# Token tiles in lots of two behind 32 turns of the identity, the slot table moved, and four combine masks stored elsewhere

## What is computed

```
xn = layernorm(x)
q  = (xn @ Wq + bq).reshape(b, h, t, dh)      # layer 0: 16 heads of 128, causal
x  = x + attn(q, k, v) @ Wo + bo + (xn @ W.T + bias + lora experts chosen by a router)
xn = layernorm(x)
# layer 1: small attention over the batch axis, and 32 experts, 4 a token, 32 slots each
shared = silu(xn @ Wsg) * (xn @ Wsu) @ Wsd * sigmoid(xn @ Wse)
xe     = tokens gathered into the slots;  ye = (silu(xe @ Wg) * (xe @ Wu)) @ Wd
out    = x + attention + shared + sum over a token's slots of weight * ye
```

## Time and profile before

| | us |
|---|---|
| median of three runs (442.76 to 443.11) | 442.82 |
| the profiled execution's own time | 443.39 |
| its span | 441.4 |
| PE busy in the span | 422.6 |
| DVE busy | 308.0 |
| ACT busy | 245.7 |
| POOL busy | 165.4 |

### The profile page before, as it was taken

The page is one execution under the profiler, slowest core; times in us unless marked ns, Lnnn a source line. Parts: engine busy times, 40 slices in busy tenths (PEclk is TensorE's granted clock), DMA queues, the critical chain, the costliest instruction groups (busy, mean ns, idle before and its releaser), DMA issues.

```text
span 441.4 us, 8830 instructions
## 1 busy us (share of the span) xinstructions
PE 422.6 (96%) x3054; PEld 377.6 (86%) x3054; DVE 308.0 (70%) x906; ACT 245.7 (56%) x670; POOL 165.4 (37%) x293
## 2 busy tenths in 40 slices
PE   2999999899999999999999999999999989999897
PEld 1788889799999999999999999899998766577797
DVE  4645675678787888887877776657688985387442
ACT  3464563577777878786967686333314613553130
POOL 3050001455555555545555530101166005999000
PEclk9999999999999999999999999999999999999999
DMA  6920011141010100101000000000099932999002
GB/s 188 225 87 1 2 48 50 51 142 50 0 50 2 35 15 12 38 1 51 1 0 3 1 1 0 26 13 12 25 313 298 310 87 67 284 299 235 1 13 83
DMA packets 41979, 34.45 MB, mean 78 GB/s; under 512 B 6689, under 2 KB 40145, under 8 KB 41937
## 3 DMA queue, kind: packets, MB, share of 16 engines
q1 hardware_dynamic: 41552, 32.85, 26.5%
q0 software_dynamic: 384, 1.05, 0.8%
HBM read 31.80 MB, written 2.10 MB: 77 GB/s over the span
## 4 chain that ended last, share of the span: by engine, by line
PE 93%; DVE 3%; ACT 2%; issue 1%; DMA 1%; POOL 0%; DVEq 0%
PE bank L921 22%; PE bank L923 22%; PE bank L922 22%; PE bank L1079 5%; PE bank L1091 3%; PE bank L1070 3%; PE bank L1312 2%; PE bank L1279 2%; PE bank L1323 2%; PE bank L1324 2%; PE bank L1121 2%; PE bank L1299 2%; DVE GT L1787 1%; PE bank L1228 1%; DMA X<-in_L_attn_x 1%
## 5 line engine op out<-in xcount | busy, mean ns | idle before, releaser
L581 POOL TENSOR_TENSOR arena<-arena,rinv 128x384 f32<-128x384 f32 x64 | 53.0, 828 | 82.0 <-DVE rinv L1565 82.0
L921 PE MATMUL bank<-XTl,WA 128*128 128x512 f32 x128 | 54.3, 424 | 2.6 <-POOL WA L548 1.7
L923 PE MATMUL bank<-XTh,WA 128*128 128x512 f32 x128 | 51.3, 401 | 0.0
L922 PE MATMUL bank<-XTh,WA 128*128 128x512 f32 x128 | 51.3, 401 | 0.0
L746 ACT ACTIVATE PT<-bank 128x256 fp32r<-128x256 f32 x64 | 24.5, 382 | 34.1 <-PE bank L1079 34.1
L1569 DVE TENSOR_TENSOR PT<-bank,PT 128x256 fp32r<-128x256 f32 x64 | 27.2, 425 | 19.7 <-ACT arena L747 19.7
L921 PE MATMUL bank<-WA,XTh 128*128 128x256 f32 x128 | 38.4, 300 | 0.6 <-DVE K L1540 0.6
L572 POOL CAST Q<-arena 128x128 fp32r<-128x128 f32 x64 | 18.7, 292 | 48.4 <-PE bank L923 48.4
L922 PE MATMUL bank<-WA,XTl 128*128 128x256 f32 x128 | 35.7, 279 | 0.0
L923 PE MATMUL bank<-WA,XTh 128*128 128x256 f32 x128 | 35.7, 279 | 0.0
L1557 DVE CUSTOM_DVE_ANT_0 arena<-bank,posm 128x128 f32<-128x128 f32 x64 | 18.1, 282 | 20.9 <-PE bank L923 20.9
(11 more groups left out here) (327 smaller groups left out, 1449.8 us busy)
## 6 DMA issues: line engine op xcount, KB each, us to landing
arena<-in_L_ffn_Wg SPq DMA_DIRECT2D x6, 704.0 KB, 8.4
arena<-in_L_ffn_Wu SPq DMA_DIRECT2D x6, 704.0 KB, 10.5
arena<-in_L_ffn_Wd SPq DMA_DIRECT2D x6, 512.0 KB, 7.8
arena<-in_L_attn_Wq SPq DMA_DIRECT2D x4, 512.0 KB, 6.5
arena<-in_L_attn_Wk SPq DMA_DIRECT2D x8, 256.0 KB, 2.7
arena<-in_L_attn_Wv SPq DMA_DIRECT2D x8, 256.0 KB, 3.2
arena<-in_L_attn_Wo SPq DMA_DIRECT2D x1, 2048.0 KB, 8.6
arena<-in_L_ffn_Wd SPq DMA_DIRECT2D x6, 192.0 KB, 7.6
```

Of the source, the lines that this page charges most:

```text
L581: pool.tensor_tensor(pr, pr, r[:, :, None].to_broadcast([P, 3, P]), ALU.mult).then_inc(s_p, 1)
L921: pe.matmul(dst, wh, xl, start=start, stop=False)
L922: pe.matmul(dst, wl, xh, start=False, stop=False)
L923: return pe.matmul(dst, wh, xh, start=False, stop=stop)
```

## The change

Seven edits, in the order of the code. (1) SP loads Wq's first two quarters in two halves each, and pieces 2 and 3 of x behind the first quarter and the bias vectors. (2) Layer norm, token turns and the splits XTh and XTl go by lots of two tiles, both feature chunks together; `stats_of` is cut into `stats_of` and `variances`. (3) PE turns the identity 32 times into bank 7 before anything else. (4) The first four query blocks are made for tokens 0 to 255 in three parts as the operands come (`first_queries`), then for tokens 256 to 511 (`queries(0)` to `queries(3)`, matmuls of 256 columns); Q_AT puts group 1's first half ahead of group 0's second. POOL takes both low halves of the first weights. (5) The router's hidden layer comes after block 11 (before: 7); ACT's R1Th follows `q_copy(10)`, DVE's R1Tl follows `q_copy(11)`. (6) `slots_of(7)` stands ahead of `shared_product(7)`, the table's copies and turn ahead of the last shared blocks, `g_low(5)` and the two last `sum_products` behind it; block 11 comes between slots 0 and 1. (7) GT's eight masks get homes of their own (two in the products' old place, one in the place of XTl's end, one over the token numbers IT), so that masks 4, 5, 6 and 7 are made earlier; shared_down(0) stands between turn(2) and down(2). Left out below: semaphores, the functions' new bodies that only rename half to lot.

```diff
+Q_AT = [(g, half, blk) for g, half in ((0, 0), (1, 0), (0, 1), (1, 1), (2, 0), (2, 1), (3, 0), (3, 1)) for blk in range(4)]
+Q_FREE = {2: 12, 3: 16, 4: 24, 5: 32}
+CHUNKS = 4
+WARM = 32
...
-EXPERT_STEPS = [("shared", (8, 1)), ("table", 0)]
-EXPERT_STEPS += [("shared", (q, k)) for q in (9, 10, 11) for k in range(2)]
-EXPERT_STEPS += [("slots", 0), ("slots", 1), ("up", 0), ("slots", 2), ("up", 1), ("turn", 0), ("slots", 3), ("up", 2),
-                 ("down", 0), ("turn", 1), ("slots", 4), ("up", 3), ("down", 1), ("turn", 2), ("down", 2), ("turn", 3), ("sd", 0),
-                 ("weigh", 0), ("split", 0), ("down", 3), ("split", 1), ("sd", 1), ("split", 2), ("split", 3),
+EXPERT_STEPS = [("table", 0), ("shared", (8, 1))] + [("shared", (q, k)) for q in (9, 10) for k in range(2)]
+EXPERT_STEPS += [("slots", 0), ("shared", (11, 0)), ("shared", (11, 1)), ("slots", 1), ("up", 0), ("slots", 2), ("up", 1), ("turn", 0),
+                 ("slots", 3), ("up", 2), ("down", 0), ("turn", 1), ("slots", 4), ("up", 3), ("down", 1), ("turn", 2), ("sd", 0),
+                 ("down", 2), ("turn", 3), ("mask", (4, 5)), ("weigh", 0), ("split", 0), ("sd", 1), ("down", 3), ("split", 1),
+                 ("split", 2), ("split", 3),
                  ("up", 4), ("slots", 5), ("split", 4), ("sd", 2), ("split", 5), ("turn", 4), ("split", 6), ("sd", 3),
-                 ("down", 4), ("mask", 0), ("up", 5), ("slots", 6), ("mask", 2), ("sd", 4), ("turn", 5), ("sd", 5), ("down", 5),
-                 ("mask", 4), ("high", 0), ("up", 6), ("slots", 7), ("high", 3), ("low", 0), ("sd", 6), ("turn", 6), ("mask", 6),
-                 ("sd", 7), ("low", 3), ("add", 7), ("down", 6), ("mix", 0), ("mix", 1), ("up", 7), ("mix", 2), ("turn", 7),
+                 ("mask", (6,)), ("down", 4), ("mask", (0,)), ("up", 5), ("slots", 6), ("mask", (1, 2)), ("sd", 4), ("turn", 5),
+                 ("mask", (3,)), ("sd", 5), ("mask", (7,)), ("down", 5),
+                 ("high", 0), ("up", 6), ("slots", 7), ("high", 3), ("low", 0), ("sd", 6), ("turn", 6), ("low", 3),
+                 ("sd", 7), ("add", 7), ("down", 6), ("mix", 0), ("mix", 1), ("up", 7), ("mix", 2), ("turn", 7),
...
-        GT = nc.alloc_sbuf_tensor_at("GT", [P, GR, N], FR, offset=at0)
+        GT = [nc.alloc_sbuf_tensor_at(f"GT{g}", [P, N], FR, offset=at)
+              for g, at in enumerate([at0 + 4 * N * k for k in range(4)] + [at0 + 4 * (28672 + N * k) for k in range(2)]
+                                     + [at_xt + 4 * (5 * C * N // 2), at1 + 4 * 2944])]
...
+            def load_x(b):
                 sp.dma_start(X[:, 2 * b:2 * b + 2, :], x_t[:, b]).then_inc(s_x[b], 16)
-                if b == 1:
-                    sp.dma_start(WQv[:, 0], wq_t[:, :, 0:512]).then_inc(s_wq[0], 16)
+
+            def load_wq_halves(g):
+                for c in range(C):
+                    sp.dma_start(WQv[:, g, c], wq_t[:, c, 512 * g:512 * g + 512]).then_inc(s_wq[g] if c else s_wqa[g], 16)
+
+            load_x(0)
+            load_x(1)
+            load_wq_halves(0)
             for i, n in enumerate(("bq", "bk", "bv")):
                 sp.dma_start(VB[16 * i:16 * i + 16, :], row(a["L0_attn_" + n], H)).then_inc(s_vb, 16)
+            load_x(2)
+            load_x(3)
+            load_wq_halves(1)
...
+            pool.wait_ge(s_wh, 1)
+            pool.tensor_tensor(WA[:, 0, 1, 512:1024], WQ[:, 512:1024], WA[:, 0, 0, 512:1024].bitcast(F32), ALU.subtract).then_inc(s_wl, 1)
...
+            deviations(0)
+            first_high(0, 0)
+            tokens_high(0)
+            deviations(1)
+            first_high(0, 1)
+            tokens_high(1)
+            first_high(1, 0)
+            deviations(2)
+            first_high(1, 1)
+            act.wait_ge(s_vc, 2)
+            q_copy(0)
+            deviations(3)
+            q_copy(2)
+            tokens_high(2)
+            q_copy(4)
+            tokens_high(3)
+            q_copy(6)
+            q_copy(8)
+            q_copy(10)
...
+            act.wait_ge(s_t, 2)
+            act.wait_ge(s_pad, 3)
+            nc.scalar.activation(R1Th[:, :, 0:HID], pb[5][:, 0:2 * HID].rearrange("p (c n) -> p c n", c=C), ACT.Copy).then_inc(s_tc, 1)
+            nc.scalar.activation(R2T[0:HID, :], pb[5][0:HID, 256:256 + E0], ACT.Copy).then_inc(s_tc, 1)
+            for g in range(1, 4):
...
-            silu(8)
...
-                if what == "shared" and n[1] == 0:
+                if what == "shared" and (n[1] == 0 or n[0] == 8):
...
+            def first_queries(i, c, part):
+                xs = slice(T * i, T * i + T)
+                for blk in range(4):
+                    wh, wl = (WA[:, 0, k].rearrange("p (c n) -> p c n", c=C)[:, c, P * blk:P * blk + P] for k in range(2))
+                    w, x = ((wh, XTh), (wh, XTl), (wl, XTh))[part]
+                    pe.matmul(pb[blk][:, xs], w, x[:, c, xs], start=(c == 0 and part == 0), stop=(c == C - 1 and part == 2))
...
+            for _ in range(WARM):
+                pe.transpose(pb[7][:, 0:P], ident[:], ident[:])
             tokens_turn(0)
+            pe.wait_ge(s_w0, 1)
+            pe.wait_ge(s_xth, 1)
+            first_queries(0, 0, 0)
+            pe.wait_ge(s_xtl, 1)
+            first_queries(0, 0, 1)
+            pe.wait_ge(s_w0, 2)
+            first_queries(0, 0, 2)
             tokens_turn(1)
-            queries(0)
-            queries(1)
-            queries(2)
+            pe.wait_ge(s_wh, 1)
+            first_queries(0, 1, 0)
+            first_queries(0, 1, 1)
+            pe.wait_ge(s_wl, 1)
+            first_queries(0, 1, 2)
+            pe.wait_ge(s_vb, 48)
+            pe.transpose(pb[6][:, 0:48], VB, ident[0:48, 0:48]).then_inc(s_t, 1)
+            for n in range(5):
+                queries(n)
             tokens_turn(2)
+            queries(5)
             tokens_turn(3)
-            pe.wait_ge(s_vb, 48)
-            pe.wait_ge(s_xtl, 1)
-            pe.transpose(pb[4][:, 0:48], VB, ident[0:48, 0:48]).then_inc(s_t, 1)
-            queries(3)
+            queries(6)
+            queries(7)
             router_turn()
-            for n in range(4, 8):
+            for n in range(8, 12):
                 queries(n)
             router_hidden()
-            for n in range(8, 16):
+            for n in range(12, 16):
                 queries(n)
...
             stats_of(0)
+            variances(0)
+            stats_of(1)
             norm(0)
+            variances(1)
             tokens_low(0)
+            norm(1)
+            stats_of(2)
             tokens_low(1)
-            dve.wait_ge(s_wh, 1)
-            nc.vector.tensor_tensor(WA[:, 0, 1, 512:1024], WQ[:, 512:1024], WA[:, 0, 0, 512:1024].bitcast(F32), ALU.subtract).then_inc(s_wl, 1)
-            stats_of(1)
-            norm(1)
             dve.wait_ge(s_t, 1)
-            nc.vector.tensor_copy(VC[:], pb[4][:, 0:48]).then_inc(s_vc, 1)
+            nc.vector.tensor_copy(VC[:], pb[6][:, 0:48]).then_inc(s_vc, 1)
             dve.wait_ge(s_vc, 1)
             nc.vector.tensor_scalar(bqs[:], VC[:, 0:H], SCALE, None, ALU.mult).then_inc(s_vc, 1)
+            variances(2)
+            second_low(0)
+            stats_of(3)
+            second_low(1)
+            variances(3)
+            norm(2)
+            q_copy(1)
+            norm(3)
             tokens_low(2)
+            q_copy(3)
             tokens_low(3)
+            q_copy(5)
+            q_copy(7)
+            q_copy(9)
...
+            q_copy(11)
+            dve.wait_ge(s_pad, 3)
+            weight_low(2, R1Tl[:, :, 0:HID], pb[5][:, 0:2 * HID].rearrange("p (c n) -> p c n", c=C), R1Th[:, :, 0:HID])
+            for g in range(1, 4):
+                w_low(g + 1, kvraw if g == 3 else wqraw(g + 1))
+                for n in range(8 * g + 1 + 4 * (g == 1), 8 * g + 8, 2):
...
+            slots_of(7)
             shared_product(7)
-            slots_of(7)
-            sum_products(6)
             dve.wait_ge(s_di, NT)
             nc.vector.tensor_copy(TK[0:TC, 512:1024], pb[5][0:TC]).then_inc(s_tkd, 1)
-            sum_products(7)
-            g_low(5)
+            sum_products(6)
 
...
-                shared_product(8)
...
-                if what == "shared" and n[1] == 1 and n[0] >= 9:
+                if what == "shared" and n[1] == 1:
                     shared_product(n[0])
                 if what == "table":
                     slot_weights()
+                    g_low(5)
+                if what == "shared" and n == (8, 1):
+                    sum_products(7)
                     sum_products(8)
+                if what == "shared" and n == (9, 1):
                     dve.wait_ge(s_sr, 9)
                     scores_less_max(1)
                 if what == "up":
```

More of the change, by code:

```diff
@@ L250, in program @@
         s_wq = [sem(f"wq_loaded{g}") for g in range(4)]
+        s_wqa = [sem(f"wq_first_half_loaded{g}") for g in range(2)]
         s_sw = sem("small_weights_loaded")
@@ L679, in weight_copy @@
                 nc.scalar.activation(dst, src, ACT.Copy).then_inc(s_tc, 1)
```

(51 more changed lines are left out.)

112 lines of the change are left out of this document (41 added, 71 removed).

## The result

The kernel before took 443.57 us in the median of 20 runs (442.54 to 444.89), the changed one 442.36 (439.52 to 442.88, 20 runs): a ratio of 0.9968, interval 0.9958 to 0.9977, some 1.4 us faster. A repeat of both on another chip gave 443.45 and 441.72, ratio 0.9959 (0.9943 to 0.9974). The forecast was 438.6. Three of the 20 runs of the changed kernel have a mean granted clock of 1.000 and took 439.52 to 441.18 us; the other 17, at 0.992 to 0.996, took 442.51 in the median.

What follows compares the result with a forecast made beforehand. PE, carrying 93% of the chain, was taken as the bound, so only its waits and half-rate matmuls counted: start 2.6 plus experts 1.6 gives 4.2 us, from 442.82 to 438.6 us; range 435.8 to 441.9.

Steps and rivals of the forecast that it cites:

- The turns and the clock: Start: identity turns raise the clock at 5.9 us, and 7.2 us go before the first token turn.
- Rival 1: Start: the identity turns don't raise the clock; the start costs 0.7 us, time 441.9 us; chance 0.24.
- The waits of the start: Up to the router's logits: the changed kernel's waits sum to 10.7 us, the router's 1.5 among them.
- What they were taken from: Start of the kernel before: of 40.66 us up to the logits, 27.4 are work and 13.3 waits and half rate.
- the term of 2.6: Start up to the router's logits: 10.7 us against 13.3, a gain of 2.6 us.
- The slot table and the first expert: Slot table and first expert: waits of 1.5 and 0.7 us go, a gain of 2.2, or 2.3 with the drain.
- The new wait at turn(4): Experts, turn(4): PE waits about 2.6 us for HE, which comes only 0.4 us earlier.
- What a wait costs: Behind turn(4) of the experts: only 0.4 us of the gain is left.
- The mix: Ahead of the mix: DVE is rid of four masks and the 1.1 us wait goes, 1.2 with the drain.
- the count: Whole kernel: the gain is counted from the runs' median of 442.82 us, 0.6 below the profiled execution.
- Rival 2: Experts, turn(4): the wait is small as DVE's chain is shorter; experts give 3.9 us, time 436.3; chance 0.13.
- Rival 3: Start: turns don't count and gaps of 0.25 to 1.5 us keep the clock low; slower, 447.5 us; chance 0.04.

Runs made afterwards that it cites:

- e8: e1's kernel with GpSimd's second query-weight subtraction held until VectorE has written both parts of the second tile's norm; 442.01 us, ratio 0.9933.
- e1: The changed kernel with shared_down(0) put back behind turn(3); 439.94 us, ratio 0.9918.
- e2: The changed kernel with 28 useless turns of the identity ahead of the experts' turn(4); 440.23 us, ratio 0.9927.
- e12: The changed kernel with VectorE's three steps of scores_weighed(1) moved behind the product of up(4); 442.44 us, ratio 0.9924.
- e10: e1's kernel with the edits of e7 and e8 together; 441.22 us, ratio 0.9905.
- e9: e1's kernel without the 32 turns of the identity; 443.72 us, ratio 0.9957.
- e11: e1's kernel run once more, unedited, on a third chip; 442.91 us, ratio 0.9937.
- e13: The changed kernel, shared_down(0) left ahead, with scores_weighed(1) late, router copies early and GpSimd's second subtraction held; 440.14 us, ratio 0.9875.
- e14: e13's kernel with shared_down(0) put back behind turn(3); 439.46 us, ratio 0.9862.
- e7: e1's kernel with R1Th moved ahead of q_copy(10) on ScalarE and R1Tl ahead of q_copy(11) on VectorE; 441.37 us, ratio 0.9925.

## Why the prediction was wrong

The sign was right and the size not: 4.2 us of gain forecast, 1.5 in the profiles (last PE instruction 438.72 against 437.20). By the steps:

- **The turns and the clock: right.** The forecast had the rise at 5.9 and the first token turn at 7.2; it was 6.3 and 7.42. Rival 1 falls: the granted clock rose while PE did nothing but turn the identity, and without the turns it rose at 13.12. The Trainium skill, "TensorE: Matmul & The Clock Gate", Part 4 on PE-mode transpose, states that the full clock doesn't engage for transposes; this trace does not agree.
- **The waits of the start: right in their sum.** 7.42 + 0.78 + 0.20 + 0.26 + 1.40 = 10.1 against 10.7 forecast, the router's 1.4 for 1.5 among them. The 0.20 is a wait for VectorE's norm that the forecast didn't have; the 0.26 stands for its 0.6 at block 5.
- **What they were taken from: a step that failed.** "So 13.3 us of the 40.66 are waits and half rate" was worked out by subtraction, with every product at its steady pace. The waits of the earlier trace rows up to there are 6.8 + 1.7 + 0.9, the half rate of the query blocks some 2: 11.4. The other 2 us or so is work slower than the steady pace, 1.3 of it in the first eight token turns, which the kernel before makes ahead of the rise. The changed kernel has 2.0 us of such work too, all behind the rise: the 24 products of 256 columns of `first_queries` took 3.4 us from start to start and not 2.8, the rest is spread over the token turns, the small turns and the blocks. The forecast counted it for the kernel before and put it at nothing for the changed one. With it the changed kernel comes to 12.1 against 13.5 (waits and slow work, from start to start), and 1.40 was measured at the logits: the term of 2.6 was 1.2 too large. 0.5 of it could have been had: POOL's second subtraction held VectorE's norm (e8), which the prediction had run side by side at no cost.
- **The slot table and the first expert: right.** 2.2 to 2.3 forecast, 4.02 - 1.43 = 2.6 measured at the first expert; both waits went.
- **The new wait at turn(4): right in place, releaser and size.** 2.6 forecast, 2.77 measured; 0.4 of the gain left, 0.6 measured (2.00 - 1.40). HE for group 4 ended 1.63 sooner (391.73 for 393.37), only 0.2 of it beyond the start's 1.40; the other 0.4 is slack that the forecast had at nothing: in the kernel before turn(4) began 0.4 behind HE's end.
- **What a wait costs: the step that failed, and the dearest.** "And only 0.4 of the gain is left behind it" priced the wait at its length. Behind it PE ran 3.41 us at the lower level, and the lead fell from 2.00 to 0.25: 1.75 us that the sum had at nothing. e1 and e2 show it from both sides: a shorter wait, or a wait filled with idle turns, and the clock stays.
- **The mix: right**, 1.2 forecast and 1.46 - 0.26 = 1.2 measured.

4.2 less 1.2 and 1.75, with 0.2 more left at turn(4), is 1.5. (The 0.3 more at the table doesn't count: the wait at turn(4) took it.) The rest of the miss is in the count: the forecast was put 0.6 under its own execution because of three runs at 442.82; the median of 20 is 443.57.

Rival 2 named the right thing in the wrong sense: it asked how short the wait at turn(4) may be and not what a long one does to the clock. Rival 3 had the mechanism, but looked for it only at the start.

## What to carry to other kernels

Price a long PE wait (here 2.6 us and more) with its length and with the chance of a stretch at half rate behind it; in the changed kernel 27 of 32 runs had it. A block that is moved ahead to cover a short wait must not be what covered a longer one: shared_down(0) covered 0.5 us at down(2) and laid bare 1.8 at turn(4). When a long wait can't be removed, turns of the identity in it keep the clock, at 0.1 us here; where another engine's order causes it, move there first (the weighing, the two router copies, GpSimd's subtraction and shared_down(0) back in its place were worth 6.2 us over the changed kernel, 441.72 to 435.54). And take a start's waits from the list of waits, not from the span less the work at its best pace.

## What was not expected of the hardware

- A wait of 2.8 us brought the clock to its lower level for 3.41 us in most runs, not in all: three of the changed kernel's first 20 runs, and two of the twelve on the other chip, show a mean clock of 1.000, and these took 439.4 to 441.4 us. The kernel before has no such wait in its two profiles. At turn(0), waits of 2.61, 2.89, 2.93, 2.94 and 2.96 us came with the fall in e12, e8, e10, e9 and e11; waits of 2.76, 2.96 and 2.98 did not, in e13, e14 and e7. So the length alone doesn't say whether the clock falls. The wait of 1.56 us at turn(4) in e13 brought no fall.
- VectorE's tensor_scalar from SBUF to SBUF, started 0.14 us after GpSimd's tensor_tensor, took 1.29 us instead of 0.41 and ended 0.14 after it. In e8 the two BATCH_NORM_STATS2 that ran beside the same subtraction kept their 0.41 to 0.42. VectorE's three splits ahead of turn(4) (two SBUF inputs each) differ in the same way: 3.39 us in the changed kernel, where GpSimd's tensor_tensor ran until 390.02 beside them, and 1.89 in e12, where GpSimd's last ended at 391.40 and they began at 391.45. If GpSimd's work is the reason, as these two profiles suggest and no run here tested, the chain that turn(4) waits for is up to 1.5 us longer for it. The Trainium skill, "GPSIMD Engine Reference", section 1 (Specifications), states that GpSimd's SBUF interfaces are shared with VectorE, with contention where VectorE's instruction runs in a 2-port mode or has two SBUF inputs; the splits agree, and in which mode the tensor_scalar ran no run here shows.
- Signals of a PE product that ended on time reached ScalarE and SyncE 3.8 us late on two of the chips, in every profile taken there.
- The rise of the clock in the kernels with turns lay between 4.9 and 7.4 us from profile to profile, and moved the first token turn with it (6.70 to 7.94 us). A single pair of profiles can therefore differ by 1 us at the start without any edit.
